# Low-rank term of a gated block on Trainium2: three half-height products per column half, or one full-height product and one on a row half of its own

## The reference, cut to what matters

```python
out = jnp.einsum('bsd,od->bso', hidden_states, W) + b
scores = x @ gate_w.T + gate_b
probs = jax.nn.softmax(scores, axis=-1)
routing_weights, selected = jax.lax.top_k(probs, TOPK)
routing_weights = routing_weights / jnp.sum(routing_weights, axis=-1, keepdims=True)
lora_outputs = jnp.stack([x @ A[:r, :].T @ B[:, :r].T for r in RANKS], axis=1)
sel = jnp.take_along_axis(lora_outputs, selected[:, :, None], axis=1)
final = jnp.sum(sel * routing_weights[:, :, None], axis=1)
return out + final.reshape(bsz, seq, -1)
```

## Time and profile before

| | us |
|---|---|
| median of 3 runs | 2142.92 |
| lowest, highest run | 2139.24, 2149.55 |
| profiled execution, its own time | 2145.24 |
| span of that execution | 2143.4 |
| granted TensorE clock, mean over the span | 0.980 of full speed |

### The profile page before, as it was taken

How to read it: one execution, slowest core, us unless ns; L and a number is a source line. 1 busy time by engine, 2 the same in 40 slices (tenths; PEclk the granted TensorE clock), 3 DMA queues, 4 the chain that set the end, 5 groups by cost and what they waited for, 6 DMA issues and landing times. The chain is left out here.

```text
span 2143.4 us, 33470 instructions
## 1 busy us (share of the span) xinstructions
PE 2002.1 (93%) x12002; PEld 1236.7 (58%) x12016; DVE 1075.2 (50%) x2012; ACT 747.4 (35%) x1560; POOL 708.4 (33%) x708
## 2 busy tenths in 40 slices
PE   7999999999999999999999689999999739999998
PEld 3468888875666666666665334444444325666665
DVE  4555555534555555554556433343443446556654
ACT  3521111223555555555555501111111233443341
POOL 0000000112655555665565400000000136666552
PEclk9999999999999999999999899999999979999999
DMA  5433333441223322224223341332321284665661
GB/s 175 143 110 108 99 108 107 119 103 40 65 62 79 98 64 61 64 64 104 69 64 94 91 125 55 79 85 49 87 73 44 69 267 136 203 197 166 201 187 53
DMA packets 313130, 223.47 MB, mean 104 GB/s; under 512 B 247968, under 2 KB 284832, under 8 KB 308816
## 3 DMA queue, kind: packets, MB, share of 16 engines
q1 hardware_dynamic: 282480, 211.23, 34.9%
q10 hardware_dynamic: 30560, 11.02, 1.9%
HBM read 170.49 MB, written 51.65 MB: 104 GB/s over the span
## 5 line engine op out<-in xcount | busy, mean ns | idle before, releaser
L815 POOL TENSOR_TENSOR b_probT<-b_exp,b_probT 128x448 f16<-128x448 f32 (+2 forms) x256 | 264.8, 1037 | 294.4 <-ACT b_probT L878 294.2
L430 POOL TENSOR_TENSOR cT<-ctx_raw,cT 128x375 f16<-128x375 f32 x256 | 221.4, 885 | 144.5 <-ACT cT L425 144.4
L654 PE MATMUL a_pr<-a_yT,proj_q_p 128*128 128x256 f16 x2016 | 223.2, 273 | 0.0
L1014 PE MATMUL b_kv_ps<-wkv_p,cT 128*128 128x384 f16 (+1 forms) x1152 | 210.8, 325 | 0.0
L654 PEld LDWEIGHTS a_pr<-a_yT,proj_q_p 128*128 128x128 f16 x2016 | 197.3, 98 | 23.4
L945 DVE TENSOR_REDUCE b_nmax<-b_mx_ps 112x2 f16<-112x974 f32 x128 | 149.6, 1169 | 106.3 <-PE b_mx_ps L1026 106.2
L1010 PE MATMUL b_kv_ps<-cT,wkv_p 128*128 128x375 f16 x1152 | 198.2, 322 | 3.7 <-PEq L447 3.7
L1051 PE MATMUL b_s_ps<-b_qT,b_kT 96*128 96x448 f16 (+5 forms) x768 | 189.4, 354 | 2.2 <-DMA b_qT<-b_nrow 2.2
L1066 PE MATMUL b_o_ps<-b_probT,b_v 128*128 128x448 f16 (+5 forms) x768 | 187.2, 351 | 3.1 <-POOL b_probT L815 3.1
L876 ACT ACTIVATE b_exp<-b_s_ps 128x448 f32<-128x448 f32 (+2 forms) x256 | 137.6, 537 | 119.9 <-PE b_s_ps L1051 112.9
L1701 PE MATMUL d_f_ps<-d_w_p,d_y3T 128*112 128x512 f16 x768 | 177.1, 385 | 0.0
(11 more groups left out here) (185 smaller groups left out, 2825.3 us busy)
## 6 DMA issues: line engine op xcount, KB each, us to landing
ctx_raw<-in_ctx_t SPq DMA_DIRECT2D x32, 1500.0 KB, 7.6
d_cn_raw<-in_ctx_nat SPq DMA_DIRECT2D x32, 512.0 KB
b_qT<-qk_scratch SPq DMA_DIRECT2D x32, 336.0 KB, 4.4
o_scratch<-b_o SPq DMA_DIRECT2D x128, 84.0 KB, 1.9
c_oT<-o_scratch SPq DMA_DIRECT2D x28, 384.0 KB, 5.0
qk_scratch<-a_heads SPq DMA_DIRECT2D x70, 144.0 KB, 2.2
d_cn_raw<-in_ctx_nat SPq DMA_DIRECT2D x16, 476.0 KB
x_scratch<-c_x SPq DMA_DIRECT2D x14, 512.5 KB, 4.7
```

The source lines that it names most:

```text
L430: pool.tensor_tensor(cT[:, p, 1, k, 0:S], ctx_raw[:, k, :], cT[:, p, 0, k, 0:S], ALU.subtract).then_inc(split_lo, 1)
L654: last = mm(pr[:, n % PR, 0:GT * P], w[:, b, k, at * P:(at + 1) * P], yT[:, g % 2, a, k, :], start=(x == 0 and k == 0), stop=(x == 2 and k ...
L815: pool.tensor_tensor(pT[0:m, c, 1, :], ex[0:m, i % 2, :], pT[0:m, c, 0, :], ALU.subtract).then_inc(p_lo, 1)
L1014: last = mm(kv_ps[0:n, k % 2, 0:KW], cT[:, p, u, d, a:a + n], wkv_p[:, w, d, KW:2 * KW], start=(r == 0), stop=(r == BLOCK - 1))
```

## The change

The leading and the trailing part of the low-rank tile are put side by side in the 128 columns of `low_p[:, 0]`, so that one turn stacks them in 128 partitions. `wb_p[:, 0]` holds the leading part of the weights twice, one copy above the other. One product of a contraction of 128 rows then gives two of the pairings (leading by leading and trailing by leading). The last pairing, leading by trailing, keeps a contraction of 64 rows; for the first column half it uses partitions 0 to 63, for the second 64 to 127, where a second copy of the leading part is put by one more VectorE operation. The weights of the term are loaded twice, once for each half of the partitions.

```diff
-            wb_p = sb("d_wb_p", [LR, 2, D], F16)
+            wb_p = sb("d_wb_p", [2 * LR, 2, D], F16)
...
-            b_in = sb("d_b_in", [LR, D], F32)
+            b_in = sb("d_b_in", [2 * LR, D], F32)
...
-            lowT = sb("d_lowT", [LR, 2, Q], F16)
+            lowT = sb("d_lowT", [2 * LR, 2, Q], F16)
...
-                sp.dma_start(b_in[:, :], wb).then_inc(small_loaded, 16)
+                for i in range(2):
+                    sp.dma_start(b_in[i * LR:(i + 1) * LR, :], wb).then_inc(small_loaded, 16)
...
-                        act.activation(lowT[:, :, :], tr[0:LR, 1, 0:2 * Q].rearrange("p (l r) -> p l r", l=2),
+                        act.activation(lowT[:, :, :], tr[:, 1, 0:2 * Q].rearrange("p (l r) -> p l r", l=2),
...
-                    dve.wait_ge(low_hi, 5 * t + 4)
+                    dve.wait_ge(low_hi, 6 * t + 4)
                     wait(dve, ltr, t)
                     dve.tensor_copy(low_p[:, 0, 0:LR], low[:, :]).then_inc(low_hi, 1)
-                    dve.wait_ge(low_hi, 5 * t + 5)
-                    dve.tensor_tensor(low_p[:, 1, 0:LR], low[:, :], low_p[:, 0, 0:LR], ALU.subtract).then_inc(low_lo, 1)
+                    dve.tensor_copy(low_p[:, 1, LR:2 * LR], low[:, :]).then_inc(low_hi, 1)
+                    dve.wait_ge(low_hi, 6 * t + 6)
+                    dve.tensor_tensor(low_p[:, 0, LR:2 * LR], low[:, :], low_p[:, 0, 0:LR], ALU.subtract).then_inc(low_lo, 1)
...
                 def low_rank(t):
                     pe.wait_ge(lowT_ready, t + 1)
                     for h in range(2):
-                        for n, (a, b) in enumerate(PASSES):
-                            last = mm(f_ps[0:Q, h, :], lowT[:, a, :], wb_p[:, b, h * HALF:(h + 1) * HALF],
-                                      start=False, stop=(n == 2))
-                        last.then_inc(ffn_done, 1)
+                        mm(f_ps[0:Q, h, :], lowT[:, 0, :], wb_p[:, 0, h * HALF:(h + 1) * HALF], start=False, stop=False)
+                    for h in range(2):
+                        at = slice(h * LR, (h + 1) * LR)
+                        mm(f_ps[0:Q, h, :], lowT[at, h, :], wb_p[at, 1, h * HALF:(h + 1) * HALF],
+                           start=False, stop=True).then_inc(ffn_done, 1)
```

More of the change, by code:

```diff
@@ L1510, in small_high @@
                 def small_high():
-                    act.wait_ge(small_loaded, 64)
+                    act.wait_ge(small_loaded, 80)
                     act.activation(wag_p[:, 0, :, :], ag_in[:, :, :], ACT.Copy, scale=WS).then_inc(small_split, 1)
@@ L1567, in small_low @@
                 def small_low():
-                    dve.wait_ge(small_loaded, 64)
+                    dve.wait_ge(small_loaded, 80)
                     dve.wait_ge(small_split, 2)
```

## The result

| | kernel before | changed kernel |
|---|---|---|
| median of 11 runs each, us | 2144.06 | 2132.37 |
| lowest, highest | 2138.73, 2149.55 | 2126.44, 2138.84 |
| profiled execution, its span | 2143.4 | 2137.0 |

The ratio is 0.9948, with a 95% interval of 0.9933 to 0.9962. That is 11.1 us faster, 8.1 to 14.4; the two medians differ by 11.7. The forecast was 7.3 us faster and 2135.6 us, with a range of 2130 to 2140.5.

What follows compares the result with a forecast made beforehand. TensorE, busy 93% of the span, was taken to bound usual slots. 13 batches x 0.56 = 7.3 us, plus 0.26 and 0.05, minus 0.3, gave 7.3 us off 2142.9: 2135.6 us, range 2130 to 2140.5.

Steps and rivals of the forecast that it cites:

- h: Step between the starts of the two 64-row low-rank matmuls on different row halves: 0.13 us, bounds 0 and 0.26.
- The bound: Usual slot of stage d: TensorE bounds it, so each nanosecond taken from the low-rank term should shorten the slot.
- The term: Low-rank term on TensorE, last dense matmul to scores: 1.18 us in place of 1.74, saving 0.56 us for each batch.
- signs of being wrong: Larger step into or out of 64-row form, usual slots keeping 23.17 us, turns always waiting for cast, collisions changing by over two.
- The batches: Of 16 low-rank terms, 13 pass the saving on (1 to 14 without 8): 13 x 0.56 = 7.3 us.
- batch 12: Slot where GpSimd's context parts delayed VectorE's scaling: collision should vanish through a later transfer, so it passes, plus 0.26 us.
- The tail: After batch 15, VectorE's `res` starts once the first column half is complete, 0.74 against 0.785 us: gains 0.05 us.
- The cast: VectorE's added 112x64 cast before the subtraction: covered in usual slots, costs 0.3 us, slot 0 and a little after stalls.
- The added load: Second weight load, 256 KB, ahead of the second four weight tiles: covered by 2.5 us, cost taken as 0.
- Rival 1: Low-rank matmuls on both row halves run at once and slot 8's collision goes: 11.6 us gain, 2131.3 us; chance 0.22.
- Rival 2: Gain spent in slot waits on GpSimd's context parts or transfers: 2139.5 to 2142 us; chance 0.14.
- Rival 3: More collisions of VectorE's scaling with GpSimd, 2.5 us each; four more typical, 2145.5 us; chance 0.06.

## Why the prediction was right, and where it was off

**The time.** The measured 2132.4 us lies in the stated range, but below the 2133.9 to 2137.3 that h at its bounds gives. The gain by the ratio is 11.1 us (8.1 to 14.4), where 7.3 was forecast; it is 0.52% (0.38 to 0.67), so it can't be told on which side of half a per cent it lies, and I gave the far side 0.24. The part that the slots show is 9.0 us. The rest isn't explained by anything in the prediction.

**The bound.** Right. In a usual slot TensorE passes on all that it saves: 0.64 us less in the term, 0.65 us less in the slot, and the 0.90 us wait unchanged.

**The term.** The mechanism was right, and two pieces were off. I put the step between the two row halves at h = 0.13 us, for the second weight load; it is 0. My one reason was that the second weights must be loaded first, and the trace shows both loads within one stretch of 0.13 us at 2025.66 us, and both matmuls right with them. The other piece went the other way: I put the step out of the 64-row form at 0.31 us as before, and out of the pair it is 0.35. A larger step out is one of the signs of being wrong that I had named (the step in stayed at 0.31), and it was small: 0.22 + 0.22 + 0.31 + 0.00 + 0.35 = 1.10 us, a saving of 0.64 us, not 0.56 and not the 0.69 of h = 0. What the Trainium skill says in TensorE: Matmul & The Clock Gate, Part 3 (Packing small matmuls), that matmuls on different row groups start about 4 ns apart, is what this trace shows (3 or 4 ns).

**The batches.** Batch 0 lost its saving to the wait behind it, as forecast (1.72 to 2.37 us). Batch 8 was no fixed loss: collisions in the loop are chance, as the other profiles show. I should have counted 14 batches, 14 x 0.644 = 9.0 us in place of 7.3, and put the collisions into the range. From this goes 0.3 us that I didn't see: the longer wait behind batch 0 is followed by a lower clock, and batch 1 passes on only half of its saving. The 0.26 us that I added for batch 12 was chance as well.

**The tail.** It gained nothing, where 0.05 us was forecast. I counted starts, 0.785 against 0.74 us, but the third matmul of the first half lasted 0.376 us before and lasts 0.420 now, so it ends at the same distance: `res` starts 1.30 us behind the last dense matmul in both kernels, and from there to the end it is 6.24 to 6.25 us before and 6.24 now.

**The cast.** A small cost in slot 0 (the wait grew from 0.41 to 0.51 us, where I had 0.2) and the cover in usual slots were right. In neither sum nor rival is that it would leave short waits of 0.2 us in some loop slots; they are part of the excess.

**The added load.** Nothing lost, as forecast, but for a wrong reason: I named the weight tiles with 2.5 us of cover, and the tile next to be late is the context tile with 1.9. The 2.5 us were a misreading too: the 9.9 us of the earlier trace rows are the median of all eight loads, and the second four by themselves land 6.1 us behind their issue in the median, the last at 1756.6, 5.2 us before ScalarE starts on them.

**Rival 1** was the closest: the halves do run at once. That its 9.0 us are also what the slots show is luck: it had 13 x 0.69, measured are 14 x 0.644. Its other part, slot 8 being freed, isn't shown as an effect of the change. **Rival 2** is out but for batch 1: with the wait of GpSimd in both kernels, all 14 batches pass their saving on. **Rival 3** had the right mechanism for the scatter and no place in the difference; its price was low where a drop of the clock follows the wait.

**What stays open.** The medians say 11.7 us, the slots 9.0. From the first scores of stage d to the end, three profiles of each kernel have a mean of 415.7 and 404.0 us, again 11.7 apart. Of this, 9.0 us are the 14 terms, 1.2 the excess (3.1 against 1.8), 1.4 the last slot, where the clock differs (8.8 against 7.3 us), and nothing the part up to batch 0's turns. The excess and the last slot scatter by 3 to 4 us from profile to profile, and with GpSimd's wait the last slots are alike (7.91 and 7.89). Whether the change has a part in these 2.6 us isn't shown; the interval holds both values.

## What to carry to other kernels

Read what a step costs from starts, multiply by the slots that aren't waiting for something else, and treat irregular slots of a single profile as a draw, not as a place. Where a contraction has 64 rows, either stacking two factors into 128 rows or putting independent products on the two row halves (with results in different PSUM banks) takes half the steps; avoiding the change of height altogether is worth a little more than the pair (0.06 us a slot here). Before adding a transfer to a full queue, look for the next consumer with the least cover, whichever tile it is; and a wait of GpSimd on VectorE, a single line, gained 5.5 us on the changed kernel and 9.0 (6.0 to 12.2) on the kernel before, half of the change or more.

## What I had not expected of the hardware

A matmul's change from 128 to 64 rows and back costs 0.09 us on the way in (a step of 0.309 us in place of 0.216) and 0.09 on the way out (0.306), 0.045 for the second step at 64 rows (0.260) or, where a pair is all there is, for the step out of it (0.350), and 0.045 between the first two matmuls behind (0.203 in place of 0.159). Two matmuls on different row halves start 3 or 4 ns apart. Waits of 1.7 to 2.2 us on TensorE were followed in several slots by a mean granted clock of 0.66 to 0.74 over the next 6 to 10 us, so such a wait can cost more than twice its length; in the first profile of the changed kernel the same 2.18 us wait was followed by full speed. Behind batch 0 the clock stayed full after 1.7 us in three profiles and fell after 2.4 us in three. And VectorE's scaling, ready at the same moment as GpSimd's first of three operations, came out behind all three.
